# Attention denominators of a graph network on one core: reciprocal on VectorE, or exp(-ln d) on ScalarE with one Newton step

## What is computed

```python
e = leaky_relu(al_s[src] + al_d[dst], 0.2)
m = segment_max(e, dst)
ex = exp(e - m[dst])
denom = segment_sum(ex, dst)
alpha = ex / (denom[dst] + 1e-16)
out = segment_sum(h[src] * alpha[:, :, None], dst)
h_next = elu(out + bias)
```

## Time and profile before

| | us |
|---|---|
| median of 3 runs | 1415.3 (1413.14 to 1418.47) |
| the profiled execution, its own time | 1416.0 |
| its span, first to last instruction | 1414.2 |
| PE busy | 1249.2 (88%) |
| DVE busy | 895.3 (63%) |
| ACT busy | 604.5 (43%) |
| chain that ended last: PE 56%, DVE 20%, ACT 9%, issue 5%, DMA 5% | |

### The profile page before, as it was taken

The page is one execution under the profiler, slowest core; times in us unless marked ns, Lnnn a source line. Parts: engine busy times, 40 slices in busy tenths (PEclk is TensorE's granted clock), DMA queues, the critical chain, the costliest instruction groups (busy, mean ns, idle before and its releaser), DMA issues.

```text
span 1414.2 us, 18321 instructions
## 1 busy us (share of the span) xinstructions
PE 1249.2 (88%) x7084; PEld 816.2 (58%) x7084; DVE 895.3 (63%) x1764; ACT 604.5 (43%) x1122; POOL 162.4 (11%) x144
## 2 busy tenths in 40 slices
PE   3773987678799899989989999999999889999996
PEld 2441554334454455444557888888854756666664
DVE  6675987898987898789854556244577623333340
ACT  4275233555743574278731355000331134444441
POOL 1000000000000000000000000500010644444422
PEclk9796998898899899999998999999799989999999
DMA  8443015133413531330165410611400277767622
GB/s 205 164 137 128 23 56 164 28 101 107 122 55 101 136 99 50 90 103 23 52 207 164 141 59 30 179 63 34 138 19 1 75 237 190 190 175 180 168 61 30
DMA packets 71010, 151.56 MB, mean 107 GB/s; under 512 B 10789, under 2 KB 34853, under 8 KB 70298
## 3 DMA queue, kind: packets, MB, share of 16 engines
q1 hardware_dynamic: 64267, 133.13, 31.3%
q0 software_dynamic: 6656, 17.26, 6.3%
HBM read 117.78 MB, written 34.59 MB: 108 GB/s over the span
## 4 chain that ended last, share of the span: by engine, by line
PE 56%; DVE 20%; ACT 9%; issue 5%; DMA 5%; SPq 2%; POOL 2%; POOLq 0%; DVEq 0%; ACTq 0%
PE PS L1692 42%; PE PS L1820 9%; DVE sb L1236 3%; DVE sb L1331 3%; ACT sb L870 3%; DVE sb L1352 2%; DMA sb<-aa_d 2%; PE PS L1815 2%; DVE sb L1208 1%; DVE sb L1261 1%; SPq L500 1%; DVE sb L1367 1%; DMA sb<-in_L_gnn_W_dram 1%; DVE sb L1360 1%; DVE sb L1405 1%
## 5 line engine op out<-in xcount | busy, mean ns | idle before, releaser
L1692 PE MATMUL PS<-sb,sb 128*125 128x384 f16 (+8 forms) x4404 | 789.4, 340 | 47.1 <-DVE sb L1213 25.2
L1692 PEld LDWEIGHTS PS<-sb,sb 128*125 128x125 f16 (+3 forms) x4404 | 545.4, 130 | 277.9 <-issue 62.9
L1820 PE MATMUL PS<-sb,sb 125*128 125x375 f16 (+1 forms) x1440 | 267.0, 347 | 0.0
L1820 PEld LDWEIGHTS PS<-sb,sb 125*128 125x128 f16 x1440 | 141.9, 99 | 122.4 <-issue 13.8
L935 ACT ACTIVATE sb<-sb 125x375 f32<-125x375 f32 (+1 forms) x150 | 81.5, 544 | 125.0 <-DVE sb L1352 124.6
L1536 DVE SCALAR_TENSOR_TENSOR sb<-sb,sb 128x2304 f16<-128x2304 f32 x27 | 68.8, 2557 | 87.8 <-ACT sb L1067 87.8
L778 POOL TENSOR_TENSOR sb<-sb,sb 125x768 f32<-125x768 f32 x10 | 18.0, 1838 | 895.0 <-DMA sb<-in_x_dram 895.0
L1352 DVE SCALAR_TENSOR_TENSOR sb<-sb,sb,sb 125x375 f32<-125x375 f32 (+1 forms) x150 | 95.3, 637 | 11.3 <-ACT sb L929 11.3
L929 ACT ACTIVATE sb<-sb,sb 125x375 f32<-125x375 f32 (+1 forms) x150 | 93.7, 628 | 7.7 <-DMA sb<-aa_d 7.7
L1722 PE MATMUL PS<-sb,sb 125*125 125x500 f16 x286 | 69.0, 398 | 30.7 <-DVE sb L1236 22.2
L1367 DVE TENSOR_TENSOR sb<-sb,sb 125x375 f16<-125x375 f32 (+1 forms) x150 | 87.8, 585 | 0.1
(11 more groups left out here) (182 smaller groups left out, 1048.9 us busy)
## 6 DMA issues: line engine op xcount, KB each, us to landing
sb<-in_L_ffn_w_dram SPq DMA_DIRECT2D x24, 1152.0 KB, 5.7
sb<-xt_d SPq DMA_DIRECT2D x37, 375.0 KB, 3.9
sb<-in_L_gnn_W_dram SPq DMA_DIRECT2D x32, 384.0 KB, 4.8
sb<-mask_d SPq DMA_DIRECT2D x20, 546.9 KB
sb<-h_d SPq DMA_DIRECT2D x10, 1000.0 KB, 6.1
h_d<-sb SPq DMA_DIRECT2D x16, 375.0 KB, 4.7
sb<-aa_d SPq DMA_DIRECT2D x5, 1093.8 KB
sb<-in_L_gnn_W_dram SPq DMA_DIRECT2D x18, 256.0 KB, 4.5
```

The lines of the kernel that those rows point to most:

```text
L1692: ins = M(out_, lhs(a), rhs(b), start=first and a + b == 0, stop=last and a == 1)
L1820: ins = M(PS[:, t, 0:n], hb[:, i, pa, 128 * c:128 * c + 128], P[:, i, pb, lo:lo + n], start=i == 0 and pa + pb == 0, stop=i == NT - 1 and ...
```

## The change

VectorE's reciprocal of a block's denominators is taken away. In its place ScalarE reads the denominators from PSUM and writes Ln of them to RDEN, then Exp of -1 times that, in place; VectorE then does one Newton step, r = r(2 - d r), in two instructions, the second of which waits for the first. ScalarE's part stands at the head of the block's first group, ahead of that group's P steps. It waits for the denominator group (`s_att`) and, since RDEN is overwritten, for the last `att_read` of the block before (`s_y1`). VectorE waits for the second activation (`s_dg`).

```diff
+            def den_guess(h, b):
+                a = NG * h + (CH + 1) * b
+                n = DB[b][1]
+                act.wait_ge(s_att, a + 1)
+                if NB * h + b:
+                    act.wait_ge(s_y1, CH * (NB * h + b))
+                A(RDEN[:, 0:n], PS[:, a % 4, 0:n], ACT.Ln).then_inc(s_dg, 1)
+                act.wait_ge(s_dg, 2 * (NB * h + b) + 1)
+                A(RDEN[:, 0:n], RDEN[:, 0:n], ACT.Exp, scale=-1.0).then_inc(s_dg, 1)
...
-                    if c >= 0:
+                    if c < 0:
+                        den_guess(h, b)
+                    else:
                         y_step(h, b, c)
                     p_steps(h, cur // 2)
...
             def den_read(h, b):
                 a = NG * h + (CH + 1) * b
                 n = DB[b][1]
-                dve.wait_ge(s_att, a + 1)
-                V.reciprocal(RDEN[:, 0:n], PS[:, a % 4, 0:n]).then_inc(s_rd, 1)
+                dve.wait_ge(s_dg, 2 * (NB * h + b) + 2)
+                link(V.scalar_tensor_tensor(RB[:, 0:n], PS[:, a % 4, 0:n], -1.0, RDEN[:, 0:n], ALU.mult, ALU.mult))
+                V.scalar_tensor_tensor(RDEN[:, 0:n], RB[:, 0:n], 2.0, RDEN[:, 0:n], ALU.add, ALU.mult).then_inc(s_rd, 1)
```

More of the change, by code:

```diff
@@ L285, in build @@
         s_dve = sem("dve_step")
-        s_keys = sem("keys_made")
+        s_keys = sem("keys_made_then_sources_in_tile")
         s_var = sem("variance_made")
@@ L303, in build @@
         s_cm = sem("pair_onehot_used")
-        s_slo = sem("sources_in_tile_made")
         s_od = sem("source_differences_made")
@@ L337, in build @@
         s_att = sem("attention_group_done")
+        s_dg = sem("denominator_inverse_guessed")
         s_rd = sem("denominator_made")
@@ L866, in differences @@
                 if q == 0:
-                    act.wait_ge(s_slo, 1)
+                    act.wait_ge(s_keys, 2)
                 a, b = OLP * q, min(OLP * (q + 1), KA)
@@ L1165, in _ @@
             dve.wait_ge(s_once, 1)
-            V.tensor_copy(SLO[:, 0:ET], PS[0:T, 7, ET:2 * ET]).then_inc(s_slo, 1)
+            V.tensor_copy(SLO[:, 0:ET], PS[0:T, 7, ET:2 * ET]).then_inc(s_keys, 1)
             link(V.tensor_copy(KEY[:, 0:ET], PS[0:T, 7, 0:ET]))
```

## The result

The changed kernel takes 1429.16 us in the median of 4 runs (1427.2 to 1431.38), against 1415.38 for the kernel before, measured beside it. The ratio is 1.0096, 95% interval 1.0072 to 1.0121: 13.8 us slower, with 10.2 to 17.1 in the interval. The profiled execution took 1427.2, the fastest of the four, and its span is 1425.4, so 11.2 more than the span before.

What follows compares the result with a forecast made beforehand. VectorE was taken to set the pace in part of the stretch, trading waits with ScalarE, though TensorE is busier. Block delays less gains 10.5, exchanges 2.4 and leaks 0.3 made 13.2 on 1415.3: 1428.5 us, range 1418 to 1440.

Steps and rivals of the forecast that it cites:

- x: At each table exchange on ScalarE: its cost past 1.30 us, between 0 and 0.35, taken as 0.17.
- the sum: Over all blocks: delays less gains 10.5 us, 14 exchanges 2.4, leaks of (1,0) and (2,0) 0.3, together 13.2 us slower.
- The term of (3,2): Head 3, block (3,2): VectorE goes on later by 2.05 us plus 2x, counted from ScalarE's end at 708.04.
- the 1.38 of (2,1): Block (2,1): ScalarE is done long before, so VectorE goes on after 1.04 in place of 2.42 us, gaining 1.38.
- Losses in full, gains in full: Heads 0 to 2: delays at (0,1), (0,2), (1,2) are paid in full; gains of 1.38 us at (1,1), (2,1) arrive in full.
- 8.66: From (2,2) through head 3: VectorE's lateness adds up to 8.66 us plus 8x, and TensorE meets it.
- rival 4: ScalarE gets ahead everywhere, as at (1,1), so VectorE's relief is paid out: 12.9 us less, 1402; chance 4%.
- The clock: TensorE runs slower behind three new or longer stalls, up to 1.6 us each on the path: 1430 to 1434; chance 12%.
- The drain: A table exchange between dependent activations drains the engine, 1.28 us in place of x each, 20 in all: 1448; chance 8%.
- Head 3 hidden: TensorE's slack in head 3 hides the 8.7 + 8x us of that stretch, leaving 3.2: 1418.5; chance 13%.
- ScalarE ahead everywhere: ScalarE leads VectorE by 3.6 + 2x us or more, so VectorE's relief is paid: 12.9 us less, 1402; chance 4%.
- No exchange: No table exchange happens; VectorE goes on 2.04 (2.50) us after ScalarE's end, sum some -7: 1409; chance 3%.

Runs made afterwards that it cites:

- the Newton step alone: The changed kernel without ScalarE's guess, RDEN a constant, VectorE's two instructions kept; 1409.17 us, ratio 0.9961 to the kernel before.
- the kernel with one set: The changed kernel with one table set holding Ln and Exp loaded once ahead of the head loop, no other loads; 1409.61 us, ratio 0.9972 to the kernel before.
- the kernel with one load a block: The changed kernel with one table set for both functions and a needless load of it ahead of each logarithm; 1418.52 us, ratio 1.0011 to the kernel before.

## Why the prediction was right, and where not

**The forecast.** 1428.5 was predicted, 1429.2 measured. The likeliest case was the one that happened, and the range held. The agreement to 0.7 us is closer than the measurement itself, whose interval is 10.2 to 17.1 us of loss.

**The place.** Right. A new wait of VectorE for ScalarE's L971 of 2.7 to 4.0 us at ten blocks, none at (1,1) and (2,1); it is under the 3 us that the prediction named at (0,2) and (1,2), 2.93 each, and at (3,2), 2.67. TensorE met the delay in head 3 earlier than forecast, not first at the last block's `p_lo` but already at 654.19, at that of (3,0), by 1.14. VectorE's step goes on 4.71 us behind ScalarE's end at the blocks of 375 columns, for 4.64 at x = 0; at (1,0), the same way, ScalarE's end is 429.76 and VectorE goes on at 434.94, 5.18 for 5.10.

**x, the price of an exchange past 1.30.** Mis-sized. I took 0.17, the middle of 0 and 0.35, and it is 0.00 to 0.02 in ScalarE's rows: the 0.35 of the earlier trace rows was, as the row itself says, a wait for TensorE. The row's releaser should have counted for more than the middle of two ends. With the measured 4.71 and 5.18, 0.07 and 0.08 more than at x = 0 (0.03 of the 0.07 by the two exchanges, 0.01 each by Ln, Exp, the hand-over and the Newton step), the sum is 10.5 + 7 x 0.07 = 11.0 and not 13.2; the next point takes off another 0.8. VectorE's timeline has 722.48 - 710.63 - 0.51 = 11.34 for the first instruction behind the last Newton step. So the sum with the mended terms, 10.2, is 0.9 short of VectorE's timeline (11.1 once its last product no longer waits the 0.22 of the earlier trace rows) and 2.1 short of the 12.34 at the W2 products. That 13.2 came so near to the measured 13.8 is partly luck: an x too large stood in for small delays that the sum did not have.

**The term of (3,2).** 2.05 + 2x in the sum. VectorE's lateness was 696.79 - 686.43 - 0.51 = 9.85 behind (3,1) and is 11.34 behind (3,2), so it was 1.5. The step that failed is the end that I took from the earlier trace rows: 708.04, behind two W2 splits in one row (x2). ScalarE's timeline of after has the guess between them, as the code has it at the head of the group:

```profile
716.95 0.83 ACT L1002 ACTIVATE sb<-sb 128x768 f16<-128x768 f32 x1
717.79 1.28 ACT L969 ACT_TABLE_LOAD   x1
...
721.30 0.83 ACT L1002 ACTIVATE sb<-sb 128x768 f16<-128x768 f32 x1
```

With one split, half of the row's 1.56, the end is 707.26 and the term 707.26 + 4.71 - 710.63 = 1.3.

**What the sum did not have.** Between 522.62 and 623.28 the marks gain 0.92 in place of the 1.38 of (2,1), so 0.5 was lost there. Behind (3,2) VectorE's lateness stays at 11.1 up to its last row in the order of the changed blocks (739.55 for 727.95 of before). The last 1.3 come from elsewhere, in ScalarE's timeline of after:

```profile
744.84 0.84 ACT L1002 ACTIVATE sb<-sb 128x768 f16<-128x768 f32 x1 [3.11 <-DMA sb<-in_L_gnn_W_dram]
751.51 0.84 ACT L1002 ACTIVATE sb<-sb 128x768 f16<-128x768 f32 x1 [5.83 <-DMA sb<-in_L_gnn_W_dram]
754.80 2.77 ACT L1002 ACTIVATE sb<-sb 128x768 f16<-128x768 f32 x3 [2.44 <-DMA sb<-in_L_gnn_W_dram]
```

In before these three started at 733.18, 738.62 and 741.95, the second after 4.61 of waiting. The first is 11.15 late with the zero mark off, the second 12.38 and the third 12.34: from the second on the W2 loads landed later than in step, and TensorE's 743.84 hangs on the third. The queue's issues of W2 loads around there are only 10.9 and 11.1 late (742.83 for 731.40, 744.46 for 732.88), so the rest arose between issue and landing. The working named the W2 loads as the latest place where TensorE would meet the delay, with no price of their own. Why they took longer was not tried.

**Losses in full, gains in full.** The first half was right: 3.18 at the end of head 0 for 1.41 + 1.58 = 2.99, and 9.7 behind 623.28 for 8.66. Also at (1,1) and (2,1) the gains came, 1.3 and 0.9 in the changed kernel for 1.38. But as a rule the second half is wrong, as the Newton step alone shows with 5.8 of 12.9 us, and rival 4 was priced by it.

**Rivals.** The clock: the mechanism was there, its price was not. Behind the stalls of head 3, TensorE's 90 matmuls from 713.16 on took 15.74 us; before, the same 90 took 14.56 with no stall ahead, from 704.21 on; the granted clock of these two stretches is 0.93 and 1.00, where 1.00 is the higher of its two levels all along. So TensorE lost 1.2 there, as this rival says; but VectorE's lateness did not grow meanwhile (11.3 before, 11.1 behind), so the loss was not on the path. The drain: refuted by all 24 loads. The Trainium skill, ScalarE: Activation LUTs, section What ACT_TABLE_LOAD costs, has about 1283 ns for the load and about 1380 ns for a drain; the trace agrees with the first (1283) and shows no room for the second between two activations. Head 3 hidden: refuted by the kernel with head 3 alone, 6.1 us slower. ScalarE ahead everywhere, 1402: its condition was not met in the changed kernel, and where it is met by force (the Newton step alone) it gives 1409, because TensorE takes over. No exchange, 1409: not what was built; in the kernel with one set it came to 1409.6, though its -7 was measured as -4 to -5, from a kernel before that was 0.4 us faster in that series. On that rival the Trainium skill, the same page, section Table sets: the hidden batching unit, is right that one set holds both functions, since a single load serves all 24 activations in the kernel with one set. What did not follow is that such a set is also the one chosen: the built program has a load ahead of each of the 24 activations.

## What to carry to other kernels

Before moving a function to an idle engine, look for table loads in the order of the built program, and count them as its first cost: 24 loads of 1.28 us turned a gain of 4 to 5 us into a loss of 14, and one explicit load of a set that holds both functions gave it back. A result from another engine should be read as late as its readers allow, behind work that is ready: in an engine that runs in order, a wait costs what stands behind it, here 8 to 12 us of 14. Between two engines in lock step a delay was paid in full here, but a relief only up to the slack of the third one; price a gain with the next engine's waits, not with the work that was removed.

## What was not expected of the hardware

A table load costs its 1283 ns and nearly nothing else: the next activation starts within 0.02 us of its end, in all 24 cases. Ln from PSUM took 484 ns for 375 columns and 587 for 500, Exp from SBUF 516 and 620; two dependent VectorE operations on 375 columns go through in 1.05 us (695.74 to 696.79), where the reciprocal took 2.50. A load of a set that is active already is not skipped: in the kernel with one load a block, its 12 needless loads take 1283 ns each like the others.

```profile
L969 ACT ACT_TABLE_LOAD x12 | 15.4, 1283 | 2.1 <-PE PS L1830 1.9
```
